# A graph network stack on one core: layer 3 placed beside the batch norm's last loop, with row scales for 32 graphs at a time

## The chip, the cores and the metric

The kernel runs on 1 core of a Trainium2 chip. The metric is the device time of one execution in microseconds (us), the median of several runs. Engines are called by the names of the profile: PE (TensorE), DVE (VectorE), ACT (ScalarE), POOL (GpSimd), SP (SyncE, whose queue issues the stores).

## The reference

128 graphs of 128 nodes with 64 features pass four pre-norm layers, each `x = x + layer(relu(layernorm(x)), adj)`. Cut to what matters here, the third and fourth:

```python
# layer 2: mean and var are taken over all 128 graphs
y = matmul(adj, h) + h;  y = y @ weight + bias
y = y / maximum(norm(y, axis=2), 1e-12)
y = ((y - mean) / sqrt(var + BN_EPS) * gamma + beta) * m     # m: node mask
x = x + relu(y)
# layer 3, every graph by itself
h = maximum(layernorm(x), 0)
messages = einsum('bij,bjh->bih', adj, h)
x = x + tanh(concat([h, messages]) @ W1 + b1) @ W2 + b2
```

## The kernel before, in words

x (all graphs, nodes on partitions) and the transposed adjacency stay in SBUF for the whole kernel. Layer 0 takes the first 1,150 us or so, then come layer 1, layer 2's products and the batch norm, then layer 3. Work from the batch norm on comes in 16 chunks of 512 columns (8 graphs, `NXC`, `GX`) or in groups of 4 graphs (`GS`), two groups (`u` = 0, 1) to a pair `i`, 16 pairs (`NI`). A chunk is thus the 8 graphs of one pair.

**The batch norm's last loop** (block from L1449) begins when `stat[:, 5, :]`, the factor per feature, is known (L1495). Per chunk DVE multiplies y by it (`scale`, L1498), POOL adds beta (`shift_chunk`, L1556), ACT applies mask and relu, one instruction per graph (L1534), then x is increased by y, on DVE for even chunks (L1513) and on POOL for odd ones (L1565), and DVE takes the statistics of x, one instruction per graph (`chunk_stats`, L279). Scale and shift run three chunks ahead (`AHEAD`). After chunk 15, `layernorm_scales` (L255 to L270, with a square root on ACT, L248, and a reciprocal on DVE, L268) makes `rstd` and `nmr` for all 128 graphs at once. The block ends there, and TensorE does nothing in this loop.

**Layer 3** (block from L1581): ACT loads the table of tanh (L1629), waits for the scales, and normalises x into `hn` (`norm_graph`, L1139, four graphs to a group). PE then makes, for a group, the sums over neighbours (L1590) and transposes (L1594) in one PSUM bank; DVE copies the bank (`copy_sums`, L1655); PE makes the hidden layer (L1600, L1601); ACT the tanh (L1642); PE the last product (L1609); DVE adds x and the bias (`update`, L1660) and the product (L1665); SP stores 4 graphs (L1685). PE and DVE run one group ahead with the sums and one behind with the product (`following`, `preceding`). Each engine's order is its program order; semaphores alone tie the engines together, and there is no planner.

Of the kernel before, what the change touches and what calls it, by code (L numbers as in the profile page):

```python
# [7 lines left out]
ALU = mybir.AluOpType  # L8
# [4 lines left out]
def gnn_stack_kernel(nc, a, out):  # L13
# [15 lines left out]
    GS = 4  # L29
# [19 lines left out]
    with ctx:  # L49
# [1366 lines left out]
        s_xn = [sem(f"x_updated_layer2_{k}") for k in range(2)]  # L1416
        s_bn2 = sem("layer3_stats_made")
        AHEAD = 3
# [15 lines left out]
        def per_feature(t):  # L1434
            return t.unsqueeze(1).broadcast_to([N, GX, F])

# [12 lines left out]
        with nc.Block() as block:  # L1449
# [16 lines left out]
            @block.vector  # L1466
            def _(dve):
                v = nc.vector
                steps = [0]

                def settled(ins):
                    steps[0] += 1
                    ins.then_inc(s_vb, 1)
                    dve.wait_ge(s_vb, steps[0])

                dve.wait_ge(s_nrm, 1)
                settled(v.tensor_scalar(ss[:, :], ss[:, :], 1e-12, None, ALU.max))
                settled(v.reciprocal(ss[:, :], ss[:, :]))
                normalise(dve, v, 0)
                dve.wait_ge(s_ms, 1)  # L1480
                dve.wait_ge(s_cutmask, 3)
                v.tensor_tensor(blk, bank[0][0:GX, :], block_mask, ALU.mult).then_inc(s_blk, 1)
                dve.wait_ge(s_tot, 1)
                settled(v.tensor_reduce(stat[:, 0, :], bank[1][:, :].rearrange("p (g f) -> p f g", f=F), AX.X, ALU.add))
                v.tensor_scalar(stat[:, 1, :], stat[:, 0, :], rcnt[:, :], None, ALU.mult).then_inc(s_mean, 1)
                dve.wait_ge(s_mean, 1)
                centre(dve, v, 0)
                dve.wait_ge(s_dms, NXC)
                v.tensor_tensor(blk, bank[2][0:GX, :], block_mask, ALU.mult).then_inc(s_blk, 1)
                dve.wait_ge(s_tot, 2)  # L1490
                settled(v.tensor_reduce(stat[:, 2, :], bank[3][:, :].rearrange("p (g f) -> p f g", f=F), AX.X, ALU.add))
                settled(v.tensor_scalar(stat[:, 3, :], stat[:, 2, :], rcnt[:, :], None, ALU.mult))
                dve.wait_ge(s_var, 1)
                settled(v.reciprocal(stat[:, 5, :], stat[:, 4, :]))
                settled(v.tensor_tensor(stat[:, 5, :], stat[:, 5, :], gamma[:, :], ALU.mult))  # L1495

                def scale(c):
                    v.tensor_tensor(g3(yc(c)), g3(yc(c)), per_feature(stat[:, 5, :]), ALU.mult).then_inc(s_ya, 1)  # L1498

                def chunk_stats(c):  # L1500
                    dve.wait_ge(s_xn[c % 2], c // 2 + 1)
                    for e in range(GX):
                        last = stats(c * GX + e)
                    last.then_inc(s_bn2, 1)

                for c in range(AHEAD):
                    scale(c)
                for c in range(NXC):
                    if c + AHEAD < NXC:
                        scale(c + AHEAD)  # L1510
                    if c % 2 == 0:
                        dve.wait_ge(s_yc, c + 1)
                        v.tensor_tensor(xc(c), xc(c), yc(c), ALU.add).then_inc(s_xn[0], 1)  # L1513
                    if c >= 1:
                        chunk_stats(c - 1)
                chunk_stats(NXC - 1)
                dve.wait_ge(s_bn2, NXC)
                layernorm_scales(dve, 5)

            @block.scalar  # L1520
            def _(act):
                act.activation(ss[:, :], ss[:, :], ACT.Sqrt).then_inc(s_nrm, 1)
                for c in range(NXC):
                    act.wait_ge(s_d[c % 2], c // 2 + 1)
                    if c >= 2:
                        act.wait_ge(s_dms, c - 1)
                    act.activation(tmp[:, 2 + c % 2, :], yc(c), ACT.Square).then_inc(s_dq, 1)
                act.wait_ge(s_vb, 5)
                act.activation(stat[:, 4, :], stat[:, 3, :], ACT.Sqrt, bias=eps_col[:, 0:1]).then_inc(s_var, 1)
                for c in range(NXC):  # L1530
                    act.wait_ge(s_yb, c + 1)
                    for b in range(c * GX, (c + 1) * GX):
                        yb = y[:, b * F:(b + 1) * F]
                        last = act.activation(yb, yb, ACT.Relu, scale=nm[:, b:b + 1])  # L1534
                    last.then_inc(s_yc, 1)
                layernorm_std(act, 5)

            @block.gpsimd
            def _(pool):
                g = nc.gpsimd  # L1540

                g.memset(block_mask, 1.0).then_inc(s_cutmask, 1)
                pool.wait_ge(s_cutmask, 1)
                g.affine_select(out=block_mask, in_=block_mask, compare_op=ALU.is_ge, fill=0.0,
                                base=0, pattern=[[1, XC]], channel_multiplier=-F).then_inc(s_cutmask, 1)
                pool.wait_ge(s_cutmask, 2)
                g.affine_select(out=block_mask, in_=block_mask, compare_op=ALU.is_ge, fill=0.0,
                                base=F - 1, pattern=[[-1, XC]], channel_multiplier=F).then_inc(s_cutmask, 1)
                pool.wait_ge(s_vb, 2)
                normalise(pool, g, 1)  # L1550
                pool.wait_ge(s_mean, 1)
                centre(pool, g, 1)

                def shift_chunk(c):
                    pool.wait_ge(s_ya, c + 1)
                    g.tensor_tensor(g3(yc(c)), g3(yc(c)), per_feature(beta[:, :]), ALU.add).then_inc(s_yb, 1)  # L1556

                for c in range(AHEAD):
                    shift_chunk(c)
                for c in range(NXC):  # L1560
                    if c + AHEAD < NXC:
                        shift_chunk(c + AHEAD)
                    if c % 2 == 1:
                        pool.wait_ge(s_yc, c + 1)
                        g.tensor_tensor(xc(c), xc(c), yc(c), ALU.add).then_inc(s_xn[1], 1)  # L1565

        s_hn3 = [sem(f"l3_h_normalised{u}") for u in range(2)]
        s_agg3 = [sem(f"l3_neighbours_summed{u}") for u in range(2)]
        s_aggs3 = [sem(f"l3_neighbour_sums_copied{u}") for u in range(2)]
        s_lin3 = [sem(f"l3_hidden_made{u}") for u in range(2)]
        s_tanh = [sem(f"l3_tanh_made{u}") for u in range(2)]
        s_dh = [sem(f"l3_product_made{u}") for u in range(2)]
        s_xb = [sem(f"l3_x_with_bias_made{u}") for u in range(2)]
        s_new = [sem(f"l3_x_updated{u}") for u in range(2)]
        s_out = [sem(f"stored{u}") for u in range(2)]

        with nc.Block() as block:  # L1581
            @block.tensor
            def _(pe):
# [42 lines left out]
            @block.scalar  # L1626
            def _(act):

                nc.scalar.activation(std[:, 0:1], eps_col[:, 0:1], ACT.Tanh)  # L1629
                act.wait_ge(s_ln, 5)  # L1630
                for u in range(2):
                    for q in range(GS):
                        norm_graph(s_hn3[u], u, GS * u, q, q == GS - 1)

                def pair(i, more):
                    for u in range(2):
                        if more:
                            act.wait_ge(s_agg3[u], i + 1)
                            for q in range(GS):
                                norm_graph(s_hn3[u], u, GS * grp(u, i + 1), q, q == GS - 1)  # L1640
                        act.wait_ge(s_lin3[u], i + 1)
                        nc.scalar.activation(hid[:, u, 0:2 * N], bank[4 * u + 1][:, 0:2 * N], ACT.Tanh,  # L1642
                                             bias=l3b1[:, 0:1]).then_inc(s_tanh[u], 1)

                with act.Fori(0, NI - 1) as i:
                    pair(i, True)
                pair(NI - 1, False)

            @block.vector
            def _(dve):  # L1650
                v = nc.vector

                def copy_sums(i, u):
                    dve.wait_ge(s_agg3[u], i + 1)
                    v.tensor_copy(msg[:, u, :], bank[4 * u][:, :]).then_inc(s_aggs3[u], 1)  # L1655

                def update(i, u):
                    if not (known(i) and i == 0):
                        dve.wait_ge(s_out[u], 16 * i)
# [56 lines left out]
```

## Time and profile before

| | |
|---|---|
| median of 3 runs | 1461.05 us (1458.61 to 1461.1) |
| the profiled execution | 1463.7 us |
| span in its trace | 1462.0 us |
| busy PE, DVE, ACT, POOL | 1316.5, 1154.9, 1105.1, 502.5 us |
| first `scale` of the last loop starts | 1327.54 us |
| first normalisation for layer 3 starts | 1376.28 us |
| granted clock of PE, mean | 0.966 |

The span runs from the first to the last instruction of the profiled execution; its own time is 1.7 us longer. Times inside the trace count from the span's start. A busy time is a sum over instructions of an engine, whose records can overlap by some tenths of a microsecond. "Granted clock" is the share of full speed (2.4 GHz) that TensorE had: 1.00 is 2.4 GHz, 0.50 is 1.2 GHz.

### The profile page before, as it was taken

To read this page: it belongs to the slowest core of one execution; us is meant where nothing else is said; L and a number is where in the kernel's file an instruction comes from. 1 tells how busy PE (TensorE), PEld (TensorE's weight loads), DVE (VectorE), ACT (ScalarE), POOL (GpSimd) and SP (SyncE) were. 2 spreads that over 40 slices of the span, in tenths; PEclk is the share of its full clock that TensorE was granted. 3 is DMA by queue.
4 is the path that set the end of the run, shared out by engine and by line. 5 is a ranking of instruction groups with operands and counts; after the bars stand their busy time and mean duration, and the time that the engine had idled before them with its cause. 6 is when DMAs were issued, how large, how long until landed. Compare 5 with 4: busy or idle time off the path is not lost. (4 is left out here: it accounts for less than half of the span.)

```text
span 1462.0 us, 41154 instructions
## 1 busy us (share of the span) xinstructions
PE 1316.5 (90%) x11243; PEld 1076.8 (74%) x11244; DVE 1154.9 (79%) x2874; ACT 1105.1 (76%) x2426; POOL 502.5 (34%) x611
## 2 busy tenths in 40 slices
PE   3999999999999999999999999997999997972398
PEld 1777777877777777777777777875889887910298
DVE  7898988899888988889888998883444445978755
ACT  4788888888888888888888888863555555916676
POOL 1343344444443344444433444431222111066400
PEclk9999999999999999999999999997999998986599
DMA  7000000000000000000000000000000000000022
GB/s 154 22 10 9 8 7 14 7 7 7 7 14 7 7 7 14 7 7 7 7 14 7 7 7 7 0 2 1 0 0 0 0 0 0 0 1 0 4 54 57
DMA packets 40925, 18.11 MB, mean 12 GB/s; under 512 B 19572, under 2 KB 40886, under 8 KB 40886
## 3 DMA queue, kind: packets, MB, share of 16 engines
q1 hardware_dynamic: 40354, 17.42, 4.8%
q8 instruction: 19, 0.31, 0.1%
q10 hardware_dynamic: 532, 0.21, 0.1%
q14 instruction: 20, 0.16, 0.0%
HBM read 13.44 MB, written 4.19 MB: 12 GB/s over the span
## 5 line engine op out<-in xcount | busy, mean ns | idle before, releaser
L723 DVE SCALAR_TENSOR_TENSOR acc<-slot_banks,acc 128x768 f32<-128x768 f32 x512 | 487.7, 953 | 79.5 <-PE slot_banks L442 70.6
L792 POOL TENSOR_TENSOR acc<-acc 128x384 f32<-128x384 f32 x128 | 128.1, 1001 | 529.1 <-DVE onediff L717 420.3
L442 PE MATMUL slot_banks<-ac_hi,work 128*128 128x192 f16 x1408 | 265.3, 247 | 27.3 <-DVE work L705 26.1
L442 PE MATMUL slot_banks<-ac_lo,work 128*128 128x192 f16 x1408 | 264.1, 246 | 0.0
L442 PEld LDWEIGHTS slot_banks<-ac_hi,work 128*128 (+1 forms) x1408 | 137.4, 98 | 98.4 <-issue 76.1
L442 PE MATMUL slot_banks<-ac_hi,onediff 128*128 128x192 f16 x1024 | 183.1, 246 | 6.4 <-DVE acc L723 5.1
L442 PE MATMUL slot_banks<-ac_lo,onediff 128*128 128x192 f16 x1024 | 182.3, 246 | 0.0
L442 PEld LDWEIGHTS slot_banks<-ac_lo,work 128*128 (+1 forms) x1408 | 138.2, 98 | 20.2 <-issue 14.5
L778 POOL TENSOR_TENSOR ac_lo<-ac,ac_hi 128x384 f16<-128x384 f32 x128 | 123.1, 961 | 49.3 <-ACT ac_hi L582 49.3
L542 ACT ACTIVATE work<-bank 128x512 f16<-128x512 f32 x256 | 130.7, 601 | 1.2 <-PE bank L353 1.2
L705 DVE TENSOR_SCALAR work<-work,slot_key 128x1024 f16 x256 | 117.9, 480 | 12.2 <-issue 3.7
L581 ACT ACTIVATE ac<-bank 128x384 f32<-128x384 f32 x128 | 62.2, 486 | 79.8 <-PE bank L402 79.8
L590 ACT ACTIVATE acc<-ac,neg_pad 128x768 f32<-128x768 f32 x128 | 119.3, 932 | 0.0
L442 PEld LDWEIGHTS slot_banks<-ac_hi,onediff 128*128 x1024 | 104.7, 102 | 16.7 <-issue 14.5
L606 ACT ACTIVATE slot_banks<-ac 128x768 f32<-128x768 f32 x127 | 103.5, 815 | 11.6
L402 PE MATMUL bank<-wac,hT 65*128 65x384 f32 x256 | 109.5, 510 | 1.7 <-ACT ac_hi L582 1.1
L599 ACT ACTIVATE work<-slot_banks 128x576 f32<-128x576 f32 x128 | 83.4, 651 | 34.9 <-PE slot_banks L442 33.3
L1218 POOL TENSOR_TENSOR adjT_all<-adjT_all,ident 128x512 f32 x32 | 39.9, 1269 | 176.1 <-PE slot_banks L1172 176.1
L442 PEld LDWEIGHTS slot_banks<-ac_lo,onediff 128*128 x1024 | 100.2, 98 | 0.0
L1139 ACT ACTIVATE onediff<-x_all,nmr,rstd 128x64 f32 (+1 forms) x256 | 90.7, 429 | 7.2 <-PE slot_banks L1310 2.9
L717 DVE TENSOR_TENSOR onediff<-work x128 | 88.6, 692 | 7.4 <-DVE work L705 0.6
L435 PE MATMUL slot_banks<-ac_hi,ident 128*128 128x384 f16 x258 | 85.1, 330 | 0.9 <-issue 0.7
(261 smaller groups left out, 3291.4 us busy)
## 6 DMA issues: line engine op xcount, KB each, us to landing
adj_in<-in_adj_dram SPq DMA_DIRECT2D x32, 256.0 KB, 2.8
out_dram<-acc SPq DMA_DIRECT2D x32, 128.0 KB, 2.0
l1w<-in_L_gnn_W_dram SPq DMA_DIRECT2D x2, 64.0 KB
l1b<-in_L_gnn_b_dram SPq DMA_DIRECT2D x2, 64.0 KB
x_all<-in_x_dram SPq DMA_DIRECT2D x4, 0.2 KB, 11.8
nm_in<-in_nodemask_dram ACTq DMA_DIRECT2D x1, 64.0 KB
w1a<-in_L_gnn_W_dram ACTq DMA_DIRECT2D x1, 48.0 KB
w1b<-in_L_gnn_W_dram ACTq DMA_DIRECT2D x1, 48.0 KB
```

The lines of the kernel that those rows point to most:

```text
L402: nc.tensor.matmul(pAC[:, 0:2 * H], hT0[:, p, q * N:(q + 1) * N], wac[:, :], start=True, stop=True)\
L435: nc.tensor.matmul(unit(pair, t, n), node, part[:, q, 0:H].unsqueeze(1).broadcast_to([N, n, H]), start=(e == 0), stop=False)
L442: last = nc.tensor.matmul(unit(pair, t, 1), hot(t), part[:, q, H:2 * H].unsqueeze(1), start=False, stop=(e == 1 and (t % SB == SB - 1 or t ...
L542: last = nc.scalar.activation(rs[:, p, :, t, :], pA3[:, :].rearrange("p (q j) -> p q j", q=GS), ACT.Copy, bias=-float(t))
L590: nc.scalar.activation(acc[:, q, :].rearrange("p (t h) -> p t h", t=SU), ac32[:, q, 0:H].unsqueeze(1).broadcast_to([N, SU, H]), ACT.Relu, ...
L606: nc.scalar.activation(unit((q + 1) % 2, 0, SU), ac32[:, q, 0:H].unsqueeze(1).broadcast_to([N, SU, H]), ACT.Copy).then_inc(s_seed, 1)
L705: nc.vector.tensor_scalar(onehot[:, ds(at, CH)], ranks.rearrange("p t j -> p (t j)"), slot_key[:, ds(key, 1)], None, ALU.is_equal).then_in ...
L717: nc.vector.tensor_tensor(onediff[:, ds(at, CH)], onehot[:, ds(at, CH)], onehot[:, ds(at_old, CH)], ALU.subtract).then_inc(s_D, 1)
L723: nc.vector.scalar_tensor_tensor(out=sums, in0=unit((q + k) % 2, 0, SU), scalar=0.0, in1=sums, op0=ALU.min, op1=ALU.add).then_inc(s_free[k ...
L778: nc.gpsimd.tensor_tensor(ac_lo[:, q, :], ac32[:, q, :], ac_hi[:, q, :], ALU.subtract)\
L792: nc.gpsimd.tensor_tensor(acc[:, q, 0:2 * H], acc[:, q, 0:2 * H], acc[:, q, 2 * H:4 * H], ALU.add)
L1139: ins = nc.scalar.activation(hn[:, u, SLOT[q] * F:(SLOT[q] + 1) * F], x[:, ds((b + q) * F, F)], ACT.Relu, bias=nmr[:, ds(b + q, 1)], scale ...
```

## The change

Layer 3's blocks are taken into the batch norm's block. The functions of PE and SP are moved as they are. On DVE, chunk c's addition to x and statistics, the scale of a later chunk, and layer 3's copies and updates stand in one unrolled order (`fold_in`); ACT's order is `fold_in_act`. DVE now adds y to x for every chunk, POOL for none. `rstd` and `nmr` are made four times, for 32 graphs each: POOL takes var to the power -0.5 and DVE adds one Newton step (`scales`), in place of ACT's square root and DVE's reciprocal. The tanh table is loaded ahead of the loop's relus.

```diff
-        AHEAD = 3
+        LEAD = 6
+        QC = 4
+        QG = QC * GX
...
+        def scale_chunk(c):
+            nc.vector.tensor_tensor(g3(yc(c)), g3(yc(c)), per_feature(stat[:, 5, :]), ALU.mult).then_inc(s_ya, 1)
...
+        def shift_chunk(pool, c):
+            pool.wait_ge(s_ya, c + 1)
+            nc.gpsimd.tensor_tensor(g3(yc(c)), g3(yc(c)), per_feature(beta[:, :]), ALU.add).then_inc(s_yb, 1)
...
+        def add_to_x(dve, c):
...
+            dve.wait_ge(s_yc, 2 * c + 2)
+            v.tensor_tensor(xc(c), xc(c), yc(c), ALU.add).then_inc(s_xn, 1)
+            dve.wait_ge(s_xn, c + 1)
+            for e in range(GX):
+                last = stats(c * GX + e)
+            last.then_inc(s_bn2, 1)
+            if c % QC == QC - 1:
+                variances(dve, c // QC)
...
+        def variances(dve, k):
...
+            v.tensor_tensor(msum[:, cols], m0, m1, ALU.add)
+            v.tensor_tensor(var[:, cols], q0, q1, ALU.add)
+            v.tensor_tensor(dif[:, cols], m0, m1, ALU.subtract).then_inc(s_lnq, 1)
+            dve.wait_ge(s_lnq, 6 * k + 1)
+            v.tensor_scalar(var[:, cols], var[:, cols], 1.0 / F, EPS, ALU.mult, ALU.add)
+            v.scalar_tensor_tensor(out=dif[:, cols], in0=dif[:, cols], scalar=0.25, in1=dif[:, cols],
+                                   op0=ALU.mult, op1=ALU.mult).then_inc(s_lnq, 1)
+            dve.wait_ge(s_lnq, 6 * k + 2)
+            v.tensor_tensor(var[:, cols], var[:, cols], dif[:, cols], ALU.add).then_inc(s_lnq, 1)
...
+        def scales(dve, k):
...
+            dve.wait_ge(s_root, k + 1)
+            v.scalar_tensor_tensor(out=error, in0=root, scalar=-0.5, in1=root, op0=ALU.mult, op1=ALU.mult)             .then_inc(s_lnq, 1)
...
+            def inverse_root(k):
+                cols = slice(k * QG, (k + 1) * QG)
+                pool.wait_ge(s_lnq, 6 * k + 3)
+                g.tensor_tensor(std[:, cols], var[:, cols], minus_half[:, :], ALU.pow).then_inc(s_root, 1)
...
+            shifts(0, LEAD)
+            inverse_root(0)
+            shifts(LEAD, QC + LEAD - 1)
+            for k in range(1, NXC // QC):
+                inverse_root(k)
+                shifts(QC * k + LEAD - 1, min(QC * k + QC + LEAD - 1, NXC))
...
+            for c in range(3):
+                scale_chunk(c)
+            for c in range(LEAD - 1):
+                add_to_x(dve, c)
+                if c + 3 <= LEAD:
+                    scale_chunk(c + 3)
+                if c == QC - 1:
+                    scales(dve, 0)
+            copy_sums(0, 0)
+            for i in range(NI):
+                copy_sums(i, 1)
+                if i > 0:
+                    update(i - 1, 1)
+                if i + LEAD - 1 < NXC:
+                    add_to_x(dve, i + LEAD - 1)
+                if i + 1 < NI:
+                    copy_sums(i + 1, 0)
+                update(i, 0)
+                if i + LEAD - 1 < NXC and (i + LEAD - 1) % QC == QC - 1:
+                    scales(dve, (i + LEAD - 1) // QC)
+                if i + LEAD + 1 < NXC:
+                    scale_chunk(i + LEAD + 1)
+            update(NI - 1, 1)
...
+            nc.scalar.activation(cnt_col[:, 0:1], eps_col[:, 0:1], ACT.Tanh)
+            for c in range(LEAD - 1):
+                masked_relu(c, 0)
+                masked_relu(c, 1)
+            norm_group(0, 0)
+            norm_group(0, 1)
+            masked_relu(LEAD - 1, 0)
+            masked_relu(LEAD - 1, 1)
+            for i in range(NI):
+                for u in range(2):
+                    if i + 1 < NI:
+                        act.wait_ge(s_agg3[u], i + 1)
+                        norm_group(i + 1, u)
+                    act.wait_ge(s_lin3[u], i + 1)
+                    nc.scalar.activation(hid[:, u, 0:2 * N], bank[4 * u + 1][:, 0:2 * N], ACT.Tanh,
+                                         bias=l3b1[:, 0:1]).then_inc(s_tanh[u], 1)
+                    if i + LEAD < NXC:
+                        masked_relu(i + LEAD, u)
```

`masked_relu(c, half)` does four graphs; `norm_group(i, u)` is four `norm_graph` and waits for the row scales at every fourth pair.

## Rows read from the trace of the kernel before

**Rows 1.** Windows (length; busy us and count of PE, PEld, DVE, ACT, POOL; clock; DMA), last stages.
```profile
1327.54:1369.50 41.96, 0.00 (x0) 0.00 (x0) 41.96 (x140) 31.31 (x128) 36.51 (x24) 0.50 0.00 1
1371.20:1376.30 5.10, 0.00 (x0) 0.00 (x0) 2.80 (x7) 1.82 (x4) 0.00 (x0) 0.50 0.00 0
1376.30:1385.60 9.30, 7.85 (x44) 7.64 (x45) 2.41 (x4) 6.33 (x19) 0.00 (x0) 0.68 0.00 0
1385.60:1455.00 69.40, 69.40 (x518) 66.47 (x517) 41.39 (x86) 51.97 (x141) 0.00 (x0) 1.00 0.24 53
```

**Rows 2.** Groups by line, the batch norm's last loop (busy us, mean ns, idle before).
```profile
L1534 ACT ACTIVATE work<-work,nm 128x64 f32<-128x64 f32 x128 | 31.3, 333 | 10.5 <-POOL work L1556 10.5
L1556 POOL TENSOR_TENSOR work<-work,beta 128x512 f32<-128x512 f32 x16 | 24.5, 1538 | 12.8 <-DVE work L1498 12.8
L279 DVE BATCH_NORM_STATS2 bn<-x_all 128x6 f32<-128x64 f32 x128 | 17.3, 205 | 0.0
```

**Rows 3.** Timeline (start, length, engine, line), first chunks of that loop.
```profile
1327.54 4.63 DVE L1498 TENSOR_TENSOR work<-work,acc 128x512 f32<-128x512 f32 x4
1328.31 6.65 POOL L1556 TENSOR_TENSOR work<-work,beta 128x512 f32<-128x512 f32 x4 [9.02 <-DVE work L1498]
1329.99 9.65 ACT L1534 ACTIVATE work<-work,nm 128x64 f32<-128x64 f32 x40 [3.39 <-POOL work L1556]
1332.10 1.75 DVE L1513 TENSOR_TENSOR x_all<-x_all,work 128x512 f32<-128x512 f32 x1
...
1336.81 1.72 POOL L1565 TENSOR_TENSOR x_all<-x_all,work 128x512 f32<-128x512 f32 x1
...
1337.33 1.75 DVE L1513 TENSOR_TENSOR x_all<-x_all,work 128x512 f32<-128x512 f32 x1
1338.49 1.71 POOL L1556 TENSOR_TENSOR work<-work,beta 128x512 f32<-128x512 f32 x1
```

**Rows 4.** Line L1498 by itself (duration ns min/median/max).
```profile
L1498 DVE TENSOR_TENSOR work<-work,acc x16: 684/946/1750, 1327.5 to 1362.6; 128x512 f32<-128x512 f32 x16
```

**Rows 5.** Timeline, the scales for all graphs, the start and the end of layer 3.
```profile
1372.22 0.29 DVE L259 SCALAR_TENSOR_TENSOR dif<-dif 128x128 f32<-128x128 f32 x1
...
1373.31 0.95 DVE L268 RECIPROCAL rstd<-std 128x128 f32<-128x128 f32 x1 [0.47 <-ACT std L248]
...
1374.87 1.28 ACT L1629 ACT_TABLE_LOAD   x1 [1.60 <-PEq L1449]
...
1376.28 2.74 ACT L1139 ACTIVATE onediff<-x_all,nmr,rstd 128x64 f32<-128x64 f32 x8
...
1382.38 0.69 DVE L1655 COPY adj_in<-bank 128x512 f32<-128x512 f32 x1 [1.41 <-PE bank L1594]
...
1454.59 0.69 DVE L1655 COPY adj_in<-bank 128x512 f32<-128x512 f32 x1 [0.69 <-PE bank L1594]
```

**Rows 6.** Groups by line, forms apart, steady part of layer 3 (1385.6 to 1455).
```profile
L1139 ACT ACTIVATE onediff<-x_all,nmr,rstd 128x64 f32 x112 | 40.0, 429 | 0.5
...
L1660 DVE TENSOR_TENSOR acc<-x_all,l3b 128x256 f32<-128x256 f32 x28 | 11.6, 415 | 0.0
L1655 DVE COPY adj_in<-bank 128x512 f32<-128x512 f32 x15 | 10.4, 692 | 10.3 <-PE bank L1594 10.3
...
L1642 ACT ACTIVATE acc<-bank,l3b 128x256 f32<-128x256 f32 x15 | 7.1, 475 | 8.9 <-PE bank L1601 8.9
...
L1665 DVE TENSOR_TENSOR acc<-slot_banks,acc 128x256 f32<-128x256 f32 x15 | 6.4, 425 | 4.3 <-PE slot_banks L1609 4.3
```

**Rows 7.** Groups by line, whole kernel: layer 0's addition from PSUM on DVE.
```profile
L723 DVE SCALAR_TENSOR_TENSOR acc<-slot_banks,acc 128x768 f32<-128x768 f32 x512 | 487.7, 953 | 79.5 <-PE slot_banks L442 70.6
```

**Rows 8.** Groups by line, POOL in layer 0.
```profile
L796 POOL TENSOR_TENSOR hm<-work 128x192 f32<-128x192 f32 x121 | 72.7, 601 | 9.5
```

**Rows 9.** Windows (columns as in rows 1) between the batch norm's two sums.
```profile
1302.00:1307.20 5.20, 1.75 (x5) 0.35 (x4) 3.09 (x5) 0.63 (x1) 1.44 (x1) 0.99 0.00 0
1307.20:1311.00 3.80, 3.80 (x6) 0.45 (x6) 3.80 (x3) 1.49 (x3) 3.80 (x4) 0.57 0.00 0
```

More of the change, by code:

```diff
@@ new lines, in variances @@
+        def variances(dve, k):
+            v = nc.vector
+            cols = slice(k * QG, (k + 1) * QG)
+            m0, q0, m1, q1 = (bn6[:, cols, t] for t in (1, 2, 4, 5))
+            dve.wait_ge(s_bn2, QC * k + QC)
+            v.tensor_tensor(msum[:, cols], m0, m1, ALU.add)
[7 more added lines that the diff above has]
+            v.tensor_tensor(var[:, cols], var[:, cols], dif[:, cols], ALU.add).then_inc(s_lnq, 1)
@@ new lines, in shifts_and_roots, with shifts @@
+        def shifts_and_roots(pool):
+            g = nc.gpsimd
+            def shifts(first, past):
+                for c in range(first, past):
+                    shift_chunk(pool, c)
+            def inverse_root(k):
+                cols = slice(k * QG, (k + 1) * QG)
+                pool.wait_ge(s_lnq, 6 * k + 3)
+                g.tensor_tensor(std[:, cols], var[:, cols], minus_half[:, :], ALU.pow).then_inc(s_root, 1)
+            g.memset(minus_half[:, :], -0.5).then_inc(s_minus, 1)
+            pool.wait_ge(s_minus, 1)
+            shifts(0, LEAD)
[4 more added lines that the diff above has]
+                shifts(QC * k + LEAD - 1, min(QC * k + QC + LEAD - 1, NXC))
@@ new lines, in fold_in_act, with masked_relu, norm_group @@
+        def fold_in_act(act):
+            def masked_relu(c, half):
+                act.wait_ge(s_yb, c + 1)
+                for b in range(c * GX + half * GX // 2, c * GX + (half + 1) * GX // 2):
+                    yb = y[:, b * F:(b + 1) * F]
+                    last = act.activation(yb, yb, ACT.Relu, scale=nm[:, b:b + 1])
+                last.then_inc(s_yc, 1)
+            def norm_group(i, u):
+                if u == 0 and i % QC == 0:
+                    act.wait_ge(s_ln3, i // QC + 1)
+                for q in range(GS):
+                    norm_graph(s_hn3[u], u, GS * grp(u, i), q, q == GS - 1)
+            nc.scalar.activation(cnt_col[:, 0:1], eps_col[:, 0:1], ACT.Tanh)
[16 more added lines that the diff above has]
+                        masked_relu(i + LEAD, u)
@@ L1464, in _ @@
                 nc.tensor.matmul(bank[3][:, :], ones[0:GX, :], blk, start=True, stop=True).then_inc(s_tot, 1)
[L1466 to L1565, printed above, removed]
@@ L1579, in gnn_stack_kernel @@
[L1579 to L1583, printed above, removed]
                 def neighbours(i, u):
@@ L1624, in _ @@
                 product(NI - 1, 1)
[L1626 to L1647, printed above, removed]
             @block.vector
@@ L1651, in _ @@
                 v = nc.vector
[L1653 to L1659, printed above, removed]
-                    v.tensor_tensor(upd[:, u, :].rearrange("p (q f) -> p q f", q=GS),
-                                    x[:, ds(GS * grp(u, i) * F, GS * F)].rearrange("p (q f) -> p q f", q=GS),
-                                    l3b2[:, :].unsqueeze(1).broadcast_to([N, GS, F]), ALU.add).then_inc(s_xb[u], 1)
-                    dve.wait_ge(s_dh[u], i + 1)
-                    dve.wait_ge(s_xb[u], i + 1)
-                    v.tensor_tensor(upd[:, u, :], bank[4 * u + 2][:, 0:GS * F], upd[:, u, :], ALU.add)\
-                     .then_inc(s_new[u], 1)
@@ L1668, in pair, with settled @@
-                def pair(i):
-                    for u in range(2):
-                        ahead, behind = following(i, u), preceding(i, u)
-                        if ahead is not None:
-                            copy_sums(*ahead)
-                        if behind is not None:
-                            update(*behind)
-                copy_sums(0, 0)
-                pairs(dve, pair)
-                update(NI - 1, 1)
+                steps = [0]
+                def settled(ins):
+                    steps[0] += 1
+                    ins.then_inc(s_vb, 1)
+                    dve.wait_ge(s_vb, steps[0])
@@ new lines, in _ @@
+                dve.wait_ge(s_nrm, 1)
+                settled(v.tensor_scalar(ss[:, :], ss[:, :], 1e-12, None, ALU.max))
+                settled(v.reciprocal(ss[:, :], ss[:, :]))
+                normalise(dve, v, 0)
+                dve.wait_ge(s_ms, 1)
+                dve.wait_ge(s_cutmask, 3)
+                v.tensor_tensor(blk, bank[0][0:GX, :], block_mask, ALU.mult).then_inc(s_blk, 1)
+                dve.wait_ge(s_tot, 1)
+                settled(v.tensor_reduce(stat[:, 0, :], bank[1][:, :].rearrange("p (g f) -> p f g", f=F), AX.X, ALU.add))
@@ new lines, in _ @@
+                dve.wait_ge(s_var, 1)
+                settled(v.reciprocal(stat[:, 5, :], stat[:, 4, :]))
+                settled(v.tensor_tensor(stat[:, 5, :], stat[:, 5, :], gamma[:, :], ALU.mult))
+                fold_in(dve)
+            @block.scalar
+            def _(act):
+                act.activation(ss[:, :], ss[:, :], ACT.Sqrt).then_inc(s_nrm, 1)
+                for c in range(NXC):
+                    act.wait_ge(s_d[c % 2], c // 2 + 1)
+                    if c >= 2:
+                        act.wait_ge(s_dms, c - 1)
+                    act.activation(tmp[:, 2 + c % 2, :], yc(c), ACT.Square).then_inc(s_dq, 1)
+                act.wait_ge(s_vb, 5)
+                act.activation(stat[:, 4, :], stat[:, 3, :], ACT.Sqrt, bias=eps_col[:, 0:1]).then_inc(s_var, 1)
+                fold_in_act(act)
@@ new lines, in _ @@
+            @block.gpsimd
+            def _(pool):
+                g = nc.gpsimd
+                g.memset(block_mask, 1.0).then_inc(s_cutmask, 1)
+                pool.wait_ge(s_cutmask, 1)
+                g.affine_select(out=block_mask, in_=block_mask, compare_op=ALU.is_ge, fill=0.0,
+                                base=0, pattern=[[1, XC]], channel_multiplier=-F).then_inc(s_cutmask, 1)
+                pool.wait_ge(s_cutmask, 2)
+                g.affine_select(out=block_mask, in_=block_mask, compare_op=ALU.is_ge, fill=0.0,
+                                base=F - 1, pattern=[[-1, XC]], channel_multiplier=F).then_inc(s_cutmask, 1)
+                pool.wait_ge(s_vb, 2)
+                normalise(pool, g, 1)
+                pool.wait_ge(s_mean, 1)
+                centre(pool, g, 1)
+                shifts_and_roots(pool)
```

58 lines of the change are left out of this document (49 added, 9 removed).

## The prediction

> **What bounds the kernel now.** I read the page's slices first: PE is near full almost everywhere, except in the last tenth. So I asked for the busy time in windows there [rows 1]. The batch norm's last loop takes 42 us in which DVE is busy throughout and PE does nothing; then 5.1 us make the scales and change the block; then layer 3 runs at PE's pace (69.4 busy of 69.4 us) with DVE at 41.4 and ACT at 52.0. The two stages use different engines and are only ordered by the layer norm of x, whose scales a graph needs for itself alone. Their two lengths, from the first scale at 1327.54 to the end at 1462.0, are 134.5 us; the change can touch nothing else. Next come the groups and the timeline of the loop [rows 2, 3]: DVE's x additions take 1.75 us, though the same form runs in 0.68 alone [rows 4].
>
> **What two tensor operations in SBUF cost each other.** POOL's addition runs from 1336.81 to 1338.53; DVE's starts at 1337.33 and ends at 1339.08, that is 0.55 to 0.7 us after POOL is done; POOL's next, at 1338.49, takes 1.71 in place of about 1.26, and would have waited for the rest of DVE's [rows 3]. One blocks the other for its whole length. DVE's operations with one input in PSUM show nothing of it: 768 columns take 953 ns in layer 0 beside a working POOL [rows 7], and the 512-column copy takes 692 ns with POOL idle, the same line through fixed cost and about 1 ns a column [rows 6]. So I let POOL block DVE's additions in SBUF, not its copies.
>
> **Step lengths.** From start to start (a record overlaps the next by about 0.08: eight norms of 0.43 take 2.74, so 0.33 each [rows 5, 6]) I take for DVE: scale 0.62; add_to_x 0.69 + 0.05 for its own semaphore + 1.02 for eight statistics (17.3 us / 128 = 0.135 and less each [rows 2]) = 1.75; copy 0.61; update 0.42 + 0.1 + 0.35 = 0.87 [rows 6]. One pair's worth in the new order is 2 copies, 2 updates, add, scale: 1.22 + 1.74 + 1.75 + 0.62 = 5.35. POOL's shift (1.26) starts 0.08 after the scale; the copy that follows covers 0.6 of it, then the bias addition of update(i-1, 1) meets it: +0.75. Five waits that stand apart: +0.1. **Pair period 6.2 us** while the loop's chunks last. ACT's pair is 2 x 4 norms (2.68), 2 tanh (0.8) and 8 relus at 0.24 (9.65 us for 40 [rows 3], 2.0) = 5.5: it fits with 0.7 to spare. PE's is 4.81 ((1454.59 - 1382.38) / 15 pairs [rows 5]): it fits. The stores are 32, as before, at most one in 2.4 us; the SP queue keeps its order and has 6.2 us where it had 4.8.
>
> **The scales, four times.** `variances` is six and `scales` four DVE operations on 32 columns. 128 columns take 0.29 [rows 5]; most of that is fixed, so 0.19 each, with the waits 1.05 and 0.85: **1.9 us per quarter**, on DVE's queue, three of the four inside the pairs. What falls away is one set for 128 columns.
>
> **The power on POOL** is not in the trace. The least is an addition of 32 columns: 192 take 0.60 [rows 8] and a free 512 take 1.26 [rows 3], so 0.27. From above: DVE's reciprocal takes 0.95 where a multiplication takes 0.29 [rows 5]; three times POOL's addition is 0.8, and a routine of many steps could be 4 us or more. I take 1.0, near the reciprocal's row. In the pairs it is hidden: between `variances` and `scales` stand a copy and an update, 1.48 us. Only the first is bare.
>
> **Order of events, t = 0 at the first scale.** First: shift 0 ends near 2.4 and relu 0 at 4.5, as in the trace, where the first x addition starts at 4.56 and is blocked to 6.3 [rows 3]; its statistics end at 7.3. Then per chunk scale 0.69, add 0.69, 0.05, statistics 1.05, and 0.3 blocked by POOL = 2.75; the fourth chunk is done at 15.5. `variances` 16.6; POOL's power 17.7 (scale 6 beside it); `scales` 18.6. From the first norm to the second group's copy is 6.1 us in the trace (1376.28 to 1382.38 [rows 5], at the low clock, which PE has here too after idling): t = 24.7. Chunk 4's addition and relu 5 go beside that. The tanh table (1.28 us [rows 5]) is loaded before the first relu has input; it and the block change (1.6 us of waiting) come off the path. Pair 0 has no update(i-1, 1) and ends at 29.6. Pairs 1 to 8: 8 x 6.2 + two quarters (pairs 2 and 6) 3.8 = 53.4, so 83.0. Pair 9 has no scale: 5.6, 88.6. Pair 10 has no scale and no shift against it, but the last quarter: 6.2 - 0.62 - 0.75 + 1.9 = 6.7, so 95.3. From there PE sets the pace: four pairs x 4.81 = 19.3, 114.6, where the last copy of a second group starts. From that copy (1454.59) to the end is 7.4 us: **t = 122.0**. Before it was 134.5: a gain of 12.5 us. The profiled execution took 1463.7, 2.6 above the median of 1461.05; taken from the median, 12.5 gives 1448.5. PE runs ahead by some tenths when DVE lets go after pair 10; I take **1448**.
>
> **Hidden work and its cover.** POOL's shifts: each must end before ACT's relu one pair later; that relu comes about 1.4 us after the scale at the earliest, so ACT waits there and spends its 0.7 of slack. If ACT's slack were gone, every tenth over would add ten tenths in all. What was POOL's share (8 additions of x) is now DVE's, 8 x 0.75, already in the sum.
>
> **The rivals.**
> 1. *The power is long.* POOL's `inverse_root` has DVE's `scales` waiting, and behind it in DVE's queue the next scale and the copy that PE needs. It costs (P - 1) at the first and (P - 1.5) at three more. With P = 4.5 us the gain of 12.5 is gone; at P = 10 the kernel is at 1448 + 9 + 25 = 1482. For it: POOL is slow per column already and nothing like it is in the trace. Against: 32 columns only. Slower: 0.08; a P of 2.5 to 5 that leaves 1453 to 1461: 0.07.
> 2. *PE loses its clock.* Before, with 1.75 us busy of 5.2, the granted clock then fell to 0.57 [rows 9]: 1.2 GHz for most of the next stretch. In the new pairs PE has 1.4 us of 6.2 free, in pieces under 1 us, and up to 2 us in the quarters. At 1.2 GHz a pair is 9.6 us of PE: 3.4 x 10 pairs = 34 more, 1482; at the low level for half of the time a pair is 7.2, +1.0 x 10, 1458. Against it: at the low level PE would be busy without a gap, and in layer 3's start it then rose within 6 us (0.68 over 9.3 us [rows 1]). 0.02 for the whole, 0.05 for the half. The Trainium skill, TensorE: Matmul & The Clock Gate, "A second HAM failure mode: psum-queue depth-cycling", says that short idle times between groups of matmuls can be enough for the clock to swing between its levels; by that rule this case would be the half, 1458.
> 3. *Hand-overs do not fit.* Each pair has six handings between PE, DVE and ACT; if the copies are blocked by POOL too (+0.6 x 9 = 5.4), or the orders leave 0.5 us a pair open, the gain is 7: 1452 to 1456. 0.15. 
> 4. *POOL hardly blocks* (the shift waits for the bias addition instead, +0.75 gone in 9 pairs) and the power is 0.3: 20 us gained, 1441. 0.08.
>
> **The numbers.** Forecast 1448, with its own band of 1444 to 1452: 0.55. The rivals as above take 0.45. Range 1441 to 1458: it leaves out the long power, the lost clock and little else. What can be told from no change is 0.2%, 2.9 us. Slower 0.10 (rival 1, the whole of rival 2); same 0.06 (ends of 1, 2); faster 0.84.
>
> **What would show it.** In the new trace: PE busy from about 1347 on; copies of one group 6.2 us apart until about 1423, then 4.8; bias additions of `update(i-1, 1)` at 1.0 to 1.2 us in place of 0.42, one in two; no idle time of DVE before `scales` but the first; POOL's power near 1 us; the end at 1449 to 1450 of the span. Wrong would be: DVE idle between additions (ACT or PE sets the period), a granted clock under 1 after 1355, a power of over 1.5 us, or a prologue longer than 24.7 us.

## The result, and the profile after

The changed kernel takes 1468.99 us (median of 9 runs), the kernel before 1461.05: ratio 1.0045, 95% interval 1.0032 to 1.0059. It is slower by 0.45%, where 12.5 us of gain were forecast. The profiled execution has a span of 1467.1 us.

The first 1,326 us do the same work in both kernels and move by several microseconds from one execution to the next. So I read every trace from the start of the first scale of the batch norm's last loop to the end of the span, **the stretch** from here on: 1462.0 - 1327.5 = 134.5 us before, 1467.1 - 1326.8 = 140.3 after, 5.8 more. The forecast was 122.0. Each stretch below is that of one profiled execution, which is not always near the median of its kernel.

Windows of the changed kernel (columns as in [rows 1]), the part before the first normalisation, the part in which both stages run, and the rest:

```profile
1326.81:1349.80 22.99, 0.00 (x0) 0.00 (x0) 15.73 (x54) 10.42 (x42) 16.49 (x8) 0.52 0.00 1
1349.80:1437.15 87.35, 66.63 (x420) 60.15 (x420) 66.29 (x212) 62.17 (x206) 27.74 (x12) 0.89 0.15 32
1437.15:1459.64 22.49, 20.70 (x137) 19.73 (x138) 11.57 (x25) 14.37 (x40) 0.00 (x0) 0.85 0.19 41
```

Counted from the first scale, layer 3's first normalisation starts after 23.0 us (1349.81) in place of 48.7, 26 us earlier: the overlap is there. But in the shared part no engine is full: DVE, which should set the pace, is busy for 66.3 of 87.4 us. The waits of the changed kernel (who waited for whom: us in total, times, longest) name the reason:

```profile
PE slot_banks L1640 <- ACT onediff L1139: 44.5, 4, 26.8
...
ACT onediff L1139 <- DVE nmr L1503: 29.1, 4, 9.3
...
DVE dif L1497 <- POOL std L1517: 17.7, 4, 5.4
```

Read from below, it is one chain: POOL makes the power, DVE's next instruction waits for it, ACT waits for the row scales, PE for ACT; four times. (Of PE's 44.5 us, 26.8 are the first wait, which begins before the last loop does, so they are no loss; the other three are 5.9 each.) The timeline of the changed kernel at the second of the four:

```profile
1371.08 0.19 DVE L1489 TENSOR_TENSOR var<-var,dif 128x32 f32<-128x32 f32 x1
...
1371.36 5.44 POOL L1517 TENSOR_TENSOR std<-var,minus_half 128x32 f32<-128x32 f32 x1 [3.68 <-DVE var L1489]
...
1372.31 0.42 DVE L1544 TENSOR_TENSOR acc<-slot_banks,acc 128x256 f32<-128x256 f32 x1
...
1376.83 0.19 DVE L1497 SCALAR_TENSOR_TENSOR dif<-std 128x32 f32<-128x32 f32 x1 [4.09 <-POOL std L1517]
...
1377.80 1.44 ACT L1139 ACTIVATE onediff<-x_all,nmr,rstd 128x64 f32<-128x64 f32 x4 [6.38 <-DVE nmr L1503]
...
1379.40 2.07 PE L1640 MATMUL slot_banks<-adjT_all,onediff 128*128 x8 [5.89 <-ACT onediff L1139]
```

A power of 32 columns takes 5.44 us. The copy and the update cover 1.4 of it, as planned; the other 4.1 stop DVE, and PE stands for 5.9. Its next eight matmuls then take 2.07 us, where the eight of the group before the wait took 1.15 (at 1370.27): they run at the low clock. Three windows of the changed kernel, the pair with the wait, the one behind it, and an undisturbed one:

```profile
1366.24:1378.22 11.98, 6.70 (x44) 5.66 (x42) 7.44 (x28) 5.39 (x19) 6.71 (x2) 0.89 0.15 33
1378.22:1384.65 6.43, 5.25 (x29) 5.08 (x30) 5.79 (x18) 5.32 (x19) 1.27 (x2) 0.68 0.09 20
1390.44:1396.39 5.95, 5.46 (x39) 4.91 (x38) 5.71 (x17) 5.54 (x20) 1.27 (x1) 1.00 0.21 45
```

The undisturbed pair is near what was forecast: 5.95 us (6.2 said), DVE busy for 5.71 of it. The bias addition that meets POOL's shift takes 1.11 us in place of 0.42, against copies of 0.68:

```profile
1390.44 0.68 DVE L1534 COPY adj_in<-bank 128x512 f32<-128x512 f32 x1
1391.04 1.11 DVE L1539 TENSOR_TENSOR acc<-x_all,l3b 128x256 f32<-128x256 f32 x1
...
1392.60 0.68 DVE L1467 TENSOR_TENSOR x_all<-x_all,work 128x512 f32<-128x512 f32 x1
...
1394.34 0.68 DVE L1534 COPY adj_in<-slot_banks 128x512 f32<-128x512 f32 x1
```

### The profile page after: what moved, and what is told of

The parts are those of the page before. It is cut to its first block and busy times, and to the rows that moved or that the text cites. A ratio compares the mean times of both kernels' runs of the same rounds, so it can differ in the third digit from the quotient of the medians.

```text
span 1467.1 us, 40785 instructions
## 1 busy us (share of the span) xinstructions
PE 1325.9 (90%) x11243; PEld 1081.8 (74%) x11244; DVE 1157.9 (79%) x2915; ACT 1100.6 (75%) x2425; POOL 509.9 (35%) x608
## 5 line engine op out<-in xcount | busy, mean ns | idle before, releaser
L1139 ACT ACTIVATE onediff<-x_all,nmr,rstd 128x64 f32<-128x64 f32 (+1 forms) x256 | 90.6, 429 | 34.3 <-DVE nmr L1503 29.1
```

Of the source, the lines that this page charges most:

```text
L1139: ins = nc.scalar.activation(hn[:, u, SLOT[q] * F:(SLOT[q] + 1) * F], x[:, ds((b + q) * F, F)], ACT.Relu, bias=nmr[:, ds(b + q, 1)], scale ...
```

## The experiments

A pair's length is taken from one copy of a second group (`copy_sums(i, 1)`) to the next. Theory A: the power's length, with what it does to PE's clock, is the whole failure. Theory B: the new order is slow by itself. Times are medians; "before" was 1461 to 1465 in these comparisons, so I give the ratio to it with its 95% interval, and the stretch of the profiled execution beside it.

**A product in the power's place.**

```diff
-                g.tensor_tensor(std[:, cols], var[:, cols], minus_half[:, :], ALU.pow).then_inc(s_root, 1)
+                g.tensor_tensor(std[:, cols], minus_half[:, :], minus_half[:, :], ALU.mult).then_inc(s_root, 1)
```

> The power on POOL is replaced by a product of the same size (32 columns) of a constant by itself; the row scales are then constants, so this kernel leaves the inverse root out. Everything else stands as in the changed kernel. Theory A (the power's length is all that failed): the product takes about 0.3 us, DVE's 17.7 us of waiting for POOL in the changed kernel go, and with them the three stretches in which PE restarts at its low clock (about 1 us each): 1469.0 - 17.7 - 3 = 1448. Theory B (the new order itself is slow: handings between engines, POOL's blocking): most of the loss stays, 1460 or more.

Measured: 1447.7 us, ratio 0.9901 (0.9863 to 0.9939), stretch 119.7. The two POOL groups of its trace:

```profile
L1461 POOL TENSOR_TENSOR work<-work,beta 128x512 f32<-128x512 f32 x16 | 22.1, 1383 | 58.0 <-DVE work L1456 58.0
L1517 POOL TENSOR_TENSOR std<-minus_half 128x32 f32<-128x32 f32 x4 | 1.3, 334 | 17.1 <-DVE var L1489 17.1
```

With 0.33 us in place of 5.44 the kernel has the forecast's time, and DVE no longer waits for POOL. Theory B falls: the order itself gains 14.8 us of stretch. The pair with the product and the one behind it, to set beside the changed kernel's 11.98 and 6.43:

```profile
1356.77:1364.56 7.79, 6.71 (x44) 5.66 (x42) 7.34 (x28) 5.40 (x19) 1.51 (x2) 1.00 0.18 39
1364.56:1370.50 5.94, 4.60 (x32) 4.24 (x33) 5.70 (x17) 5.85 (x21) 1.26 (x1) 1.00 0.17 37
```

The 20.6 us between the two kernels lie in three places: 4.8 before the first pair, 4.2 in each of three pairs with a power, and 3.3 in the pairs behind these. The first two are nearly the whole of DVE's waits for the power (17.7 us); the third is the clock, as an experiment below shows.

**The power twice.**

```diff
                 pool.wait_ge(s_lnq, 6 * k + 3)
+                g.tensor_tensor(rstd[:, cols], var[:, cols], minus_half[:, :], ALU.pow)
                 g.tensor_tensor(std[:, cols], var[:, cols], minus_half[:, :], ALU.pow).then_inc(s_root, 1)
```

> The power on POOL is done twice (the first into a buffer that is overwritten later). Theory A: each of the four waits grows by one power, 5.4 us, with nothing to hide it: 1469.0 + 4 x 5.4 = 1490.6. Theory B (the wait is mostly covered, the loss lies elsewhere): under 1480.

Measured: 1488.59 us, ratio 1.0171 (1.0134 to 1.0208), stretch 164.3, which is 24.0 more than the changed kernel's: 4 x 5.4 and 2.4 on top. That is from the longest of its four executions; by the medians it is 19.6 more, where 21.6 were expected. A second power lengthens each pair that has one by 5.4 us (11.98 to 17.37): nothing covers it. The same from the waits of its trace:

```profile
DVE dif L1497 <- POOL std L1518: 39.2, 4, 10.8
```

**Eight columns of power.**

```diff
-                g.tensor_tensor(std[:, cols], var[:, cols], minus_half[:, :], ALU.pow).then_inc(s_root, 1)
+                few = slice(k * QG, k * QG + 8)
+                g.tensor_tensor(std[:, cols], minus_half[:, :], minus_half[:, :], ALU.mult).then_inc(s_minus, 1)
+                pool.wait_ge(s_minus, k + 2)
+                g.tensor_tensor(std[:, few], var[:, few], minus_half[:, 0:8], ALU.pow).then_inc(s_root, 1)
```

> The power is taken of 8 of the 32 columns in each quarter, a product of a constant fills the rest (a power less than wanted: 24 of 32 row scales are constants, and the true inverse root is left out there). If the power's time goes by columns (5.44 us / 32 = 0.17 each) it takes about 1.5 us; if most of it is fixed, 4 us or more. By theory A the stretch from the first scale to the end is then near the product kernel's 119.7, since 1.5 us and the product's 0.3 just fit under the copy and the update that cover it: 121 to 123.

Measured once only: 1453.42 us beside 1465.43 for the kernel before on the same chip; stretch 124.0.

```profile
L1520 POOL TENSOR_TENSOR std<-var,minus_half 128x8 f32<-128x8 f32 x4 | 6.6, 1660 | 0.3
L1518 POOL TENSOR_TENSOR std<-minus_half 128x32 f32<-128x32 f32 x4 | 1.3, 334 | 17.1 <-DVE var L1489 17.1
```

1.66 us for 8 columns and 5.44 for 32 give 3.78 / 24 = 0.158 us a column and 0.4 fixed, if two sizes make a line. The product and this power, 2.0 us together, are already longer than their cover of 1.4, and DVE waits for POOL for 3.8 us in all; the stretch is 1 us above the range expected.

**Matmuls to keep the clock.**

```diff
+                            if u == 1 and i % QC == QC - 1:
+                                for _ in range(5):
+                                    nc.tensor.matmul(bank[7][:, :], ident[:, :], x[:, 0:512], start=True, stop=True)
                             neighbours(*ahead)
...
-                pairs(pe, pair)
+                for i in range(NI):
+                    pair(i)
```

> The changed kernel, with five matmuls of 512 columns into an unused bank put before the three groups of neighbour sums that wait for new row scales (pairs 3, 7, 11); TensorE's loop over pairs is unrolled for it. Theory (what the product kernel did not account for, 140.3 - 119.7 = 20.6 us against 17.7 of waiting, is the low clock after each of the waits): TensorE idles under 2 us there, its clock stays at 1.00 in the stretches that showed 0.55 to 0.76, and the stretch from the first scale to the end falls by 2 to 4 us, 1465 to 1467. Rival (the rest is refilling of the pipeline, whatever the clock): no change, 1469, or up to 2 us more if the matmuls last longer than the wait.

Measured: 1464.85 us, ratio 1.0012 (0.9998 to 1.0026) where the changed kernel has 1.0045; stretch 136.7, 3.6 less. The timeline of PE (a matmul of 512 f32 columns leaves two records, so x10 are the five) and the two windows that answer to the changed kernel's:

```profile
1373.91 4.46 PE L1669 MATMUL bank<-x_all,ident 128*128 128x512 f32 x10
1379.85 1.16 PE L1640 MATMUL slot_banks<-adjT_all,onediff 128*128 128x128 f32 x8 [1.48 <-ACT onediff L1139]
```

```profile
1366.82:1378.78 11.96, 10.99 (x54) 7.39 (x52) 7.42 (x27) 5.49 (x20) 6.71 (x2) 1.00 0.15 33
1378.78:1384.73 5.95, 4.73 (x32) 4.36 (x33) 5.71 (x17) 5.86 (x21) 1.26 (x1) 1.00 0.10 22
```

The pair with the wait is as long as ever (11.96), but the clock stays at 1.00, the eight matmuls take 1.16 us, and the pair behind is 5.95 in place of 6.43. So the rest of the loss was PE's clock: 17.7 + 3.6 is 21.3 against the 20.6 to be explained. It is not spread evenly: the pairs behind the three waits shorten by 0.5, 0.8 and 2.5 us (6.43, 6.72 and 7.96 to 5.95, 5.95 and 5.50). Behind the last wait DVE is busy for only 2.9 of the 7.96 us, and PE sets the pace; behind the first DVE is busy for 5.8 of 6.43, so its work hides most of what PE loses. The Trainium skill, TensorE: Matmul & The Clock Gate, "HAM oscillation — how this bites in real kernels", says that idle gaps throttle the array and that the work behind each runs cold. It tells this of waits for DMA; here PE waits for ACT, and after its three waits of 5.9 us the trace agrees (2.07 us in place of 1.16 for eight matmuls).

**The scale ahead of the statistics.**

```diff
-        def add_to_x(dve, c):
+        def add_to_x(dve, c, ahead=None):
...
             v.tensor_tensor(xc(c), xc(c), yc(c), ALU.add).then_inc(s_xn, 1)
+            if ahead is not None and ahead < NXC:
+                scale_chunk(ahead)
             dve.wait_ge(s_xn, c + 1)
...
-                    add_to_x(dve, i + LEAD - 1)
+                    add_to_x(dve, i + LEAD - 1, i + LEAD + 1)
...
-                if i + LEAD + 1 < NXC:
-                    scale_chunk(i + LEAD + 1)
```

> The changed kernel with DVE's scale of a later chunk put between the addition to x and its eight statistics, so that POOL's shift runs beside the statistics, which have one input, and no longer beside the bias addition of the update. Theory (POOL's blocking is the size read in the trace): nine bias additions fall from 1.1 to 0.42 us, 0.7 x 9 = 6 us if DVE sets the pair period, at least 3 us if ACT (5.5 us a pair) takes over: 1463 to 1466. Rival: ACT's relu waits for the shift, which it now gets earlier by 2 us, so nothing is lost there; if blocking is no cost, 1469.

Measured: 1468.76 us, ratio 1.0042 (1.0024 to 1.006), stretch 141.2 (in the longest of its ten executions): no gain, where 3 to 6 us were expected. Its bias additions are short, and between two waits the pairs take 5.2 to 5.3 us (copies of one group at 1389.05, 1394.37, 1399.57). The groups by line, and its waits:

```profile
L1541 DVE TENSOR_TENSOR acc<-x_all,l3b 128x256 f32<-128x256 f32 x28 | 11.6, 415 | 0.0
...
ACT onediff L1139 <- DVE nmr L1505: 33.4, 4, 11.2
...
DVE dif L1499 <- POOL std L1519: 17.9, 4, 5.6
```

The blocking had the size said: the bias addition is 0.7 us shorter, and a pair that took 5.95 us takes 5.20. But only four pairs are clear of the waits; they gain 2.0 us together (22.96 to 21.01). ACT now waits 33.4 us for the scales where it waited 29.1, the pair with the power is 12.4 us in place of 12.0, and the one behind it 8.1 in place of 6.4, at a granted clock of 0.58 in place of 0.68. These take back what the four pairs gained. Why the clock was lower behind the same power, no run isolates.

**The power given time, twice.** First with seven chunks of lead, scale and shift a chunk further ahead, and DVE's Newton step after the next addition:

```diff
-        LEAD = 6
+        LEAD = 7
...
                     add_to_x(dve, i + LEAD - 1)
+                if i + LEAD - 1 <= NXC and i + LEAD - 1 > QC and (i + LEAD - 1) % QC == 0:
+                    scales(dve, (i + LEAD - 1) // QC - 1)
...
+                if i + LEAD + 2 < NXC:
+                    scale_chunk(i + LEAD + 2)
...
+            shifts(0, QC + 3)
+            for k in range(NXC // QC):
+                inverse_root(k)
+                shifts(QC * k + 7, min(QC * k + 11, NXC))
```

> The power is kept, but given time: seven chunks of lead in place of six, scale and shift one chunk further ahead, and DVE takes up the Newton step one chunk later (after the next addition to x) than in the changed kernel. Theory A: three waits of 4.1 us are gone and the first is covered by two chunks (4.7 of 5.4 us), the first layer 3 group starts about 3 us later than without any wait: 1450 to 1453. Theory B: 1460 or more. A third: POOL, busy for 5.4 us with the power, hands its shifts over late and ACT's relu waits: 1455 to 1460.

Measured: 1461.4 us, ratio 0.9988 (0.9968 to 1.0008), stretch 132.7. DVE still waited 3.1 us, because the order that I gave POOL put the power behind a shift whose scale DVE had not yet issued: it began 3.4 us after the variances were ready (1371.39, 1368.02). By its time that is theory B's, but DVE's waits for the power went on (10.0 us in all), so it doesn't decide between them. Then with that shift behind the power (`shifts(0, 7)`, root 0, `shifts(7, 10)`, and so on):

> As the kernel that gives the power more time, but POOL takes it up before the shift of the next chunk and not after it; in that kernel the power began 3.4 us after the variances were ready and DVE still waited 3.1 us. Theory A: it begins at once and the three later waits are under 0.5 us; stretch 132.7 - 3 x 3 = 124, 1451 to 1453. Third theory (POOL hands its shifts over late): DVE does not wait for the power but for ACT's relu, 1456 or more.

Measured: 1456.12 us, ratio 0.9956 (0.9938 to 0.9973), stretch 126.0; expected 124. By its time alone this is the third theory's, but nowhere in this trace's stretch does DVE wait for a relu of ACT. DVE's wait for the power is 0.29 us here (4.4 in all four, 2.6 of them at the first), and the step behind it is blocked by a shift:

```profile
1374.89 1.25 DVE L1497 SCALAR_TENSOR_TENSOR dif<-std 128x32 f32<-128x32 f32 x1 [0.29 <-POOL std L1517]
1376.17 0.19 DVE L1499 TENSOR_TENSOR dif<-dif,var 128x32 f32<-128x32 f32 x1
```

The same power as in the changed kernel, with one chunk more of lead and its result taken up later, turns 1.0045 into 0.9956.

This trace shows one thing more. POOL's power runs from 1369.41 to 1374.85, and DVE's additions with both inputs in SBUF keep their length beside it (L1456 at 1370.71 and L1467 at 1372.77 take 0.68 us each, L1539 at 1371.91 takes 0.41). In the changed kernel it is the same (L1539 at 1371.79, 0.42 us). What holds DVE up is POOL's shift, not POOL's being busy.

**No power: the root on DVE.** `after` lets each operation signal and has DVE wait for it.

```diff
-                g.tensor_tensor(std[:, cols], var[:, cols], minus_half[:, :], ALU.pow).then_inc(s_root, 1)
...
+            after(v.tensor_scalar(root.bitcast(I32), var[:, cols].bitcast(I32), 1, None, ALU.arith_shift_right))
+            after(v.tensor_scalar(root.bitcast(I32), root.bitcast(I32), -1.0, 1597463007.0, ALU.mult, ALU.add))
+            for step in range(2):
+                after(v.scalar_tensor_tensor(out=error, in0=root, scalar=-0.5, in1=root, op0=ALU.mult, op1=ALU.mult))
+                after(v.tensor_tensor(error, error, var[:, cols], ALU.mult))
+                after(v.scalar_tensor_tensor(out=root if step < 1 else rstd[:, cols], in0=error, scalar=1.5, in1=root,
+                                             op0=ALU.add, op1=ALU.mult))
```

> The power on POOL is replaced by a first value from the bits of the variance (an integer shift and a subtraction, on DVE) and two Newton steps on DVE: five more operations of 32 columns with a wait each, 5 x 0.22 = 1.1 us per quarter, none on POOL. Theory A: the stretch from the first scale to the end is that of the product kernel (119.7) plus 4 x 1.1 less the 0.3 of the product each: about 123, against 134.5 before: 1450. Theory B (handing to POOL and back costs little, DVE's queue is what matters, so every DVE operation there stalls TensorE and its clock): 1455 or more.

Measured: 1456.51 us, ratio 0.9959 (0.9945 to 0.9973), on theory B's side; stretch 126.6 (in the shortest of its six executions, 1450.69), above the 123 expected. The nine dependent operations stand 0.22 us apart (1363.88 to 1365.66), as said; but PE stands for 2.81 us until ACT has the scales, and the clock falls (windows of this kernel):

```profile
1366.00:1370.00 4.00, 2.45 (x11) 2.46 (x12) 3.86 (x11) 3.92 (x13) 1.26 (x1) 0.60 0.07 16
1370.00:1375.00 5.00, 5.00 (x24) 4.54 (x23) 2.99 (x9) 2.97 (x10) 1.26 (x1) 0.64 0.18 39
```

In this one execution PE stands for 2.81 us twice, before 1367.55 and before 1395.83, and the clock does not answer alike: behind the first wait eight matmuls take 2.07 us and the pair 7.92, behind the second 1.15 us and 5.94 at a clock of 1.00. So whether a wait of this length costs the clock can change from one wait to the next, and a stretch from one execution holds such luck.

Then with the scale ahead of the statistics as well:

> As the kernel with the root on DVE, and the scale of a later chunk stands between the addition to x and its statistics. In the kernel with that order alone the pair period fell from 5.95 to 5.25 us, but each wait for the power stayed. Theory: with no power the nine pairs keep their 0.7 us each: 6 us less than the kernel with the root on DVE, stretch about 117, 1444. Rival (ACT, with 5.4 us of work a pair, or the quarter's operations, take the place): 1448 to 1450.

Measured: 1448.68 us, ratio 0.9914 (0.9892 to 0.9936). That is the rival's 1448 to 1450, not the theory's 1444. The profiled execution was the longest of six, 1456.93 us at a mean clock of 0.969, and its stretch is 126.0, with a low clock behind all three waits; four of the others took 1446.6 to 1448.9 at 0.976 to 0.978. So this stretch may well be longer than that of the median execution. Then with three idle-time matmuls, as above:

> As the kernel with the root on DVE and the scale ahead of the statistics, plus three matmuls of 512 columns ahead of each group that waits for new row scales. In that kernel's trace TensorE had 2.05 us of work in the 5 us around the first such wait and the clock then fell to 0.71; its stretch from the first scale to the end is 126.0 us. Theory (the low clock after each of the three waits costs about 1.2 us, as five matmuls showed in the changed kernel, 3.6 in all): 122.5, 1445. Rival (what is left there is DVE's queue of 3 us of small operations, and the matmuls only stand in its place): 126, 1449.

Measured: 1448.01 us, ratio 0.9895 (0.9873 to 0.9917), stretch 119.8, 6.2 less than in that long execution. The pair with a wait and the one behind it, without the matmuls (first fence) and with them (second):

```profile
1364.37:1372.74 8.37, 6.79 (x44) 5.79 (x42) 7.63 (x32) 4.98 (x18) 1.27 (x1) 1.00 0.21 47
1372.74:1379.98 7.24, 5.46 (x29) 5.23 (x30) 5.11 (x17) 5.63 (x19) 1.27 (x1) 0.76 0.08 18
```

```profile
1362.24:1370.62 8.38, 7.82 (x47) 6.38 (x46) 7.63 (x33) 5.09 (x18) 1.27 (x1) 1.00 0.21 47
1370.62:1376.34 5.72, 5.60 (x33) 4.18 (x32) 5.01 (x17) 5.54 (x19) 1.27 (x1) 1.00 0.10 23
```

The first pair is the same to 0.01 us; without the matmuls the second is 1.5 us longer, twice, and 3.0 behind the last wait. Against an execution in which the clock fell three times, that is what the matmuls are worth. Both medians are near 1448, and their intervals overlap, so a gain of the kernel's time is not shown.

**Seven chunks of lead with the root on DVE.**

```diff
-        LEAD = 6
+        LEAD = 7
...
-                if i + LEAD - 1 < NXC and (i + LEAD - 1) % QC == QC - 1:
-                    scales(dve, (i + LEAD - 1) // QC)
+                if QC < i + LEAD - 1 <= NXC and (i + LEAD - 1) % QC == 0:
+                    scales(dve, (i + LEAD - 1) // QC - 1)
```

> As the kernel with the root on DVE and the scale ahead of the statistics, with seven chunks of lead in place of six, and the row scales made one pair after their variances and still one pair before ACT needs them. Theory (the loss left is the wait of ACT for the scales, 17.0 us in four, which takes TensorE with it): three of the four waits go, and the clock stays; the fourth, before the first group, grows by a chunk of 2.4 us. Stretch 126.0 - 3 x 3 + 2.4 = 119 to 120, 1442. Rival (DVE's work sets the length, wherever the scales stand): 124 to 126, 1448.

Measured: 1449.34 us, ratio 0.9907 (0.9887 to 0.9927), stretch 121.1: the median near the rival's 1448, the stretch between the two expectations. ACT's wait for the scales falls from 17.0 to 11.1 us, but twice the pair behind still takes 7.3 us at a clock of 0.76 or 0.77.

The best by its ratio is the kernel with root and order changed and the three matmuls: 0.9895 of the kernel before, and faster than the changed kernel too. From the same kernel without the matmuls (0.9914) and from the one with seven chunks of lead (0.9907) it can't be told apart.

## Why the prediction was wrong

- **The step that failed** is the term "the power on POOL": taken as 1.0 us, measured 5.44 (5.87 the first time). I let DVE's reciprocal stand for it, an operation of another engine. The upper end, "4 us or more", was written down and then used as if it ended at 4. This was rival 1, with its break-even at P = 4.5, at a chance of 0.08 for slower. Its own formula, (P - 1) + 3 (P - 1.5), gives 4.4 + 3 x 3.9 = 16.1, so 1464.1; measured 1468.99. (By the same formula a P of 5 is 1462.5, where the rival says that 2.5 to 5 leave 1453 to 1461.)
- **What the formula missed** is rival 2 as a consequence of rival 1: after each wait of 5.9 us PE ran at the low clock too. I had weighed the two apart. The matmuls show 3.6 us of it.
- **The cover** of 1.48 us was right: DVE's idle time was 4.1, which is 5.44 less 1.4 with the semaphores.
- **The pair period**: forecast 6.2, measured 5.95. POOL's blocking, forecast 0.75, measured 0.69 (1.11 less 0.42), and only where both inputs are in SBUF; the PSUM copy stays at 0.68 (1366.24, beside the shift at 1366.40). Rivals 3 and 4 did not come. "One blocks the other" was read from additions alone, and POOL's power does not do it.
- **The start**: forecast 18.6 to the first scales, measured 1349.77 - 1326.81 = 23.0, of which 4.9 is the power's excess (5.87 less 1.0). Another 1.1 is a shift that blocked the first Newton operation (1347.84, 1.26 us in place of 0.19), which the sum did not have; the rest was 1.6 shorter than forecast (a chunk took 2.34 us, forecast 2.75). From the first norm to the second group's copy: 5.8, forecast 6.1. From the last such copy to the end: 7.5, forecast 7.4. PE's own pace is 4.84 in the last three pairs, forecast 4.81; but the fourth from the end takes 7.96 at a clock of 0.58, and 5.61 in the product kernel.
- **The sum without that term** was right: the product kernel's stretch is 119.7, forecast 122.0, and its median 1447.7, forecast 1448. With the product's 0.33 us the forecast sum would be 121.3. That the medians agree to 0.3 us is in part luck: the kernel before took 1464.9 in that comparison, so by the ratio 14.5 us were gained where 12.5 were forecast. The order of events was right, one size was off, and the clock behind it was left out; the range did not hold because its upper end came from a P of at most about 4.
- **The new operations on DVE** took 0.19 us each and a quarter's ten 1.9 us, as forecast. Table load: at 1325.88, before the first relu had input, as forecast.

## What to carry to other kernels

An operation that no trace shows is the term to bound first, and a cross-engine analogy is no bound: time the operation by itself first, or keep the chances of every size open. If a queue waits for another engine's slow result, put the take-up where the result is due, not where it is written; here one chunk more of lead and a later take-up were worth 13 us (1468.99 to 1456.12), without making anything faster. And a wait that reaches TensorE can be paid twice, in the wait and in the clock behind it.

## What the runs showed of the hardware

- GpSimd's power of f32, 128 partitions: 5.44 us for 32 columns, 1.66 for 8, so 0.158 us a column and 0.4 fixed by these two sizes; its product of 32 columns takes 0.33. The power's first call took 5.87.
- The power on GpSimd did not hold up VectorE's additions in SBUF (0.42 and 0.68 us beside it, as alone); GpSimd's addition of 512 columns did (1.11 in place of 0.42).
- Three matmuls of 512 columns, in time that was idle anyway, kept the granted clock at 1.00; the pairs behind were 1.5 to 3.0 us shorter than in the traced execution without them.
- TensorE idle for 2.81 us, twice in one execution: the clock was low behind the first and full behind the second.
- ACT's table load came 0.02 us after the activation before it and cost 1.28 us to the next one (1325.88 to 1327.17), with no further pause.
